# Products of constants in unused rows of a PSUM bank, at the end of positions in which TensorE has little to do

## The reference

```python
h = _L0_tok_ref(x, L0_tok_W)
h = h + _L0_attn_ref(_layernorm(h), ...)   # Toeplitz mixing along the sequence, by FFT
h = h + _L0_ffn_ref(_layernorm(h), ...)    # product keys -> k, v; then causal attention
h = h + _L1_attn_ref(_layernorm(h), ...)   # one head of full attention
h = h + _L1_ffn_ref(_layernorm(h), ...)    # 8 experts, top 2
```

```python
k = jnp.einsum('bnhk,bnhkd->bnhd', kv_scores, keys_table[ind])
v = jnp.einsum('bnhk,bnhkd->bnhd', kv_scores, values_table[ind])
sim = jnp.where(causal, jnp.einsum('bihd,bjhd->bhij', q, k), neg)
out = jnp.einsum('bhij,bjhd->bhid', softmax(sim), v)
```

## Time and profile before

| | |
|---|---|
| median of 3 runs | 3515.86 us (3515.56 to 3523.73) |
| profiled execution | span 4054.8 us; no other time of this execution is recorded, and nothing is recorded around the span |
| TensorE busy, products | 3145.7 us, 78% of the span, 9980 records |
| VectorE busy | 2896.5 us, 71% |
| ScalarE busy | 2063.6 us, 51% |
| GpSimd busy | 2009.3 us, 50% |
| granted clock of TensorE, mean | 0.865 |

### The profile page before, as it was taken

How to read it: one execution, slowest core, us unless ns; L and a number is a source line. 1 busy time by engine, 2 the same in 40 slices (tenths; PEclk the granted TensorE clock), 3 DMA queues, 4 the chain that set the end, 5 groups by cost and what they waited for, 6 DMA issues and landing times.

```text
span 4054.8 us, 40659 instructions
## 1 busy us (share of the span) xinstructions
PE 3145.7 (78%) x9980; PEld 1450.3 (36%) x9980; DVE 2896.5 (71%) x9977; ACT 2063.6 (51%) x4521; POOL 2009.3 (50%) x2084
## 2 busy tenths in 40 slices
PE   4895165687878787988887777889786778787898
PEld 2452022243434242433343333334343333333434
DVE  5435877778787777787788787877878787864423
ACT  3112145555555555555557565556585646555422
POOL 3000166666666665555555565565555565655200
PEclk9997577897989897988989888989888989888887
DMA  0121012121212121212121211111111212111000
GB/s 13 40 70 29 28 45 65 42 63 43 63 43 64 42 62 40 62 41 59 38 57 44 56 51 52 49 53 50 50 49 46 58 47 56 46 55 41 21 3 3
DMA packets 87160, 186.50 MB, mean 46 GB/s; under 512 B 40231, under 2 KB 42188, under 8 KB 86926
## 3 DMA queue, kind: packets, MB, share of 16 engines
q0 software_dynamic: 66560, 135.40, 12.7%
q1 hardware_dynamic: 20366, 48.53, 3.8%
HBM read 182.74 MB, written 1.05 MB: 45 GB/s over the span
## 4 chain that ended last, share of the span: by engine, by line
DVE 38%; PE 25%; issue 10%; another core or an unknown queue 9%; ACT 7%; DVEq 0%; ACTq 0%
DVE mx_W L1455 8%; PE mx_acc L1098 6%; PE mx_O L1110 5%; DVE mx_KVs L1623 4%; PE mx_area L1144 3%; ACT mx_GT L1360 3%; DVE mx_mx_part L1643 2%; PE mx_D L1088 2%; ACT mx_W L1292 2%; DVE mx_hot L1589 1%; DVE mx_mx L1643 1%; DVE mx_hot L1588 1%; DVE mx_S L1473 1%; DVE mx_row L1591 1%
## 5 line engine op out<-in xcount | busy, mean ns | idle before, releaser
L1070 POOL DMA_INDIRECT mx_G<-in_kv_table,mx_slot_i x2048 | 1977.6, 966 | 1781.5 <-DVE mx_W L1455 646.6
L1098 PE MATMUL mx_acc<-mx_W,mx_table 128*128 128x512 f32 x2048 | 1198.4, 669 | 0.4 <-ACT mx_kvT L1299 0.4
L1455 DVE SCALAR_TENSOR_TENSOR mx_W<-mx_D,mx_W 128x512 f32<-128x512 f32 x1024 | 704.2, 688 | 482.2 <-remote 221.3
L1292 ACT ACTIVATE mx_W<-mx_D 128x512 f32<-128x512 f32 x1024 | 607.0, 593 | 528.9 <-PE mx_D L1088 251.2
L1360 ACT ACTIVATE mx_GT<-mx_G,mx_slot_w 128x128 f32<-128x128 f32 x2048 | 758.5, 494 | 17.7 <-DVE mx_KVs L1623 13.4
L1088 PE MATMUL mx_D<-mx_U,mx_pick_b 96*128 96x512 bf16 x1024 | 437.7, 427 | 163.1 <-DVE mx_W L1455 127.3
L1098 PEld LDWEIGHTS mx_acc<-mx_W,mx_table 128*128 128x128 f32 x2048 | 443.0, 218 | 197.9 <-issue 119.5
L1316 ACT ACTIVATE mx_PT<-mx_area 128x512 f32<-128x512 f32 x480 | 247.5, 516 | 456.0 <-PE mx_area L1148 120.8
L1110 PE MATMUL mx_O<-mx_PT,mx_KVs 128*65 128x512 f32 (+3 forms) x768 | 333.7, 518 | 106.8 <-ACT mx_OT L1308 72.5
L1124 PE MATMUL mx_area<-mx_KTa,mx_QTa 64*128 64x512 f32 (+3 forms) x384 | 207.4, 625 | 229.0 <-DVE mx_mx_part L1643 138.2
L1623 DVE TENSOR_REDUCE mx_KVs<-mx_GT 128x128 f32<-128x2048 f32 x128 | 291.8, 2280 | 7.3 <-ACT mx_GT L1360 6.6
(11 more groups left out here) (350 smaller groups left out, 4604.3 us busy)
## 6 DMA issues: line engine op xcount, KB each, us to landing
mx_table<-in_kv_dense SPq DMA_DIRECT2D x64, 512.0 KB
mx_G<-in_kv_table,mx_slot_i POOLq DMA_INDIRECT x2048
cv_table<-in_c_idft SPq DMA_DIRECT2D x12, 512.0 KB, 3.2
cv_table<-in_c_dft SPq DMA_DIRECT2D x6, 512.0 KB, 3.3
cv_table<-in_c_idft SPq DMA_DIRECT2D x4, 256.0 KB, 3.2
out_h<-mx_xc SPq DMA_DIRECT2D x4, 256.0 KB
mx_G<-in_c_pick SPq DMA_DIRECT2D x1, 528.0 KB
st_h<-in_tok_W,em_ids POOLq DMA_INDIRECT x32
```

Source lines behind the costliest of these rows:

```text
L1070: pool.indirect_dma_start(G[g % RING][:, r, :], None, a["kv_table"], bass.IndirectOffsetOnAxis(slot_i[n % 2][:, k, r:r + 1], 0))\
L1098: pe.matmul(acc[:, :], table[:, tile, :], W[c % TILE_RING][:, :], start=(tile == 0), stop=(tile == TILES - 1)).then_inc(applied, 1)
L1292: act.activation(W[c % TILE_RING][:, :], D_ps[c % 3][:, :], ACT.Exp).then_inc(p_done, 1)
L1455: dve.scalar_tensor_tensor(W[c % TILE_RING][:, :], D_ps[c % 3][:, :], 0.0, W[c % TILE_RING][:, :], ALU.is_ge, ALU.mult).then_inc(w_done, 1)
```

## The change

A function `streamed(cnt, q)` adds up, from the timetable alone, how many columns TensorE streams in position `q` (a bfloat16 product of 512 columns counts 512, a float32 one 4 x 512). At the end of each position of slots 1 to 16, the new `spare_rows` then issues as many products of constants as bring that number near `STEADY` = 4800: `(4800 - streamed) // 512` of them, between none and four. Each has a constant of 96 rows by 32 columns as weights, streams 512 columns of another constant in bfloat16, and writes rows 96 to 127 of the bank `O_ps`, whose rows 0 to 64 hold the attention outputs. Nothing reads what they write. They wait for no semaphore and signal none.

```diff
+STEADY = 4800
...
+def streamed(cnt, q):
+    c = q - SLOT
+    total = 0
+    if 0 <= c + 3 < PAIRS * SLOT:
+        total += HALF * (2 if corner_of(tile_of(c + 3)[2])[3] else 1)
+    if 0 <= c < PAIRS * SLOT:
+        total += 4 * HALF
+    for use in area_uses(q - 2):
+        if use in cnt.weigh:
+            total += 4 * (HALF - piece(use)[2])
+    for use in area_uses(q)[:1]:
+        kind, _, _, r = use
+        if kind == "S":
+            total += 4 * ((r + 1) * P if r < 4 else HALF if r % 2 == 0 else ((r - 4) // 2 + 1) * P)
+        elif kind == "ST":
+            total += 4 * (HALF - piece(use)[2])
+        else:
+            total += 4 * HALF
+    key = cnt.x_at.get(divmod(q, SLOT))
+    if key is not None:
+        total += {"U": 8 * P, "post": 4 * P, "KK": 4 * P, "l1x": 4 * P, "l2x": 4 * P, "l2r": 4 * NB * E,
+                  "Y": 16 * (D + 1), "l1y": 16 * (D + 1)}.get(key[0], 4 * HALF)
+    return total
...
+            def spare_rows(count):
+                flat = pick_b[:, :, :].rearrange("p a c -> p (a c)")
+                for _ in range(count):
+                    pe.matmul(O_ps[96:P, :], pick_b[:, 0, 0:32], flat[:, 0:HALF], start=True, stop=True,
+                              skip_group_check=True)
...
                 if 0 <= c < PAIRS * SLOT and late:
                     apply_dense(c)
+                if 0 <= c < PAIRS * SLOT:
+                    spare_rows(max(0, STEADY - streamed(cnt, q)) // HALF)
```

## The result

| | before | changed |
|---|---|---|
| median of 4 runs | 3516.99 us | 3561.48 us |
| profiled execution, span | 3519.1 us (run `d1_before`, see below) | 3557.1 us |
| ratio of the times | | 1.0125, 95% interval 1.0112 to 1.0137 |
| TensorE busy | 2966.9 us, 84% | 3147.4 us, 88% |
| VectorE busy | 2888.9 us, 82% | 2891.6 us, 81% |

The change is 44.5 us slower. The prediction was 3500 us, 0.45% faster; the measured time is 1.5 us outside its range for 8 in 10 (3445 to 3560).

The account below looks back on a forecast made before the run. VectorE held 38% of the chain, TensorE 25%, with 847 us at half clock as target. Gain 40 less cost 27 gave -13 us, about -11 to -12 scaled, plus 4 us from earlier slot starts: 3500 us (8 in 10: 3445 to 3560).

Parts of the forecast that it names:

- Together 27 us: Cost of spare products on TensorE's chain: seven slots at 3.1 us make 22, the other eight at 0.6 make 5.
- I take off a fifth: 40 us: Gain from fuller clock in slots 2 to 16: 49 us, less a fifth because the clock falls behind pauses.
- -13: Net change in us on the profiled execution: 40 of clock gain against 27 of cost.
- scaled by 3515.86 / 4054.8 = 0.87: Whole kernel: the sum on the 4054.8 us profiled execution, times 0.87 for timed runs, about -11 to -12 us.
- so a further one costs (1.25 - 0.38) / 4 = 0.218 us at full clock: TensorE's time per spare product, from existing 512-column products of constants; 1067 of them make 232 us.
- The weight load of 98 ns is hidden in this pace, and the new one has 32 columns, not 128: Spare products on TensorE: weight loading adds nothing; by the skill's rule exposed cost would rise some 12 us.
- 11 x 0.218 x 0.16 = 0.4 us: Cost per slot in third quarters: 11 products, with TensorE on the chain for 16%.
- 32 x 0.218 x 0.034 = 0.2 us a slot: Cost in second quarters: about 32 products, TensorE on the chain for 3%, VectorE setting the pace.
- The first quarters' term: First quarters of slots 2 to 6, 10 and 14: 34 products, TensorE 34% of chain, 2.5 us a slot.
- Rival D: Slower: products expose TensorE's catching up in first quarters of slots 2 to 6, 10, 14; 3546 us (3527 to 3575), chance 0.28.
- Rival C: Nothing: clock ignores 32-column products, or is near full in timed runs and products sit in waits; 3510 to 3526 us, chance 0.12.
- Rival B: Large gain: ScalarE and VectorE follow TensorE's half-clock lateness, products fall into waits; 3455 us (3430 to 3475), chance 0.15.

Follow-up runs that it names:

- d1_before: The kernel before, repeated without edit for its profile on a chip without pauses: 3520.9 us, mean clock 0.913.

## Why the prediction was wrong

**The step that failed: the balance of "Together 27 us" of cost and "I take off a fifth: 40 us" of gain.** The cost took TensorE's share of the chain as the share of the products that is exposed. Without pauses, by the table above, 142 of some 297 us fell into waits and some 155 did not, 24 of them in slot 1, 49 in the first quarters, 47 in the second and 35 in the third. The gain was larger than forecast too, some 107 us, but smaller than this cost: +48 in place of -13. In the chain itself the spare products stand with 142 us where the prediction had 27. The direction of the clock was right: 32 columns of weights do hold it, as expected from the earlier trace rows (slot 1 from 0.80 to 0.95). But it gives back most where TensorE had waits to fill, and there it is not the engine that is waited for.

**The base: the sum "is made against the 4054.8 us of the profiled execution and then scaled by 3515.86 / 4054.8 = 0.87".** That most of the difference is pauses, and that the timed runs lack them, was right, but to scale a sum by 0.87 supposes that what stays keeps its proportions. It does not. Without the pauses the time at half clock is 382 us and not 847, and TensorE holds 38% of the chain and not 25%. This is not what turned the sign: on chips with the pauses, the kind that the rows come from, the forecast was -13 us, and the change measured +31, its first quarters alone +30 and +23 where the prediction has 17.5 us of cost and 7 x 26 x 0.34 / 2 = 31 of gain.

**The price: "so a further one costs (1.25 - 0.38) / 4 = 0.218 us at full clock" and "The weight load of 98 ns is hidden in this pace, and the new one has 32 columns, not 128".** The pace, 0.216 us, was right. What the row with five idle products couldn't show was the switch: those have 128 columns, as their neighbours have. 0.19 us a group, 67 us in 352 groups, is a term that was missing, 29% on top of the 232 us. It was part of the loss only where TensorE had no wait to fill, and what it cost the kernel by itself was not measured without pauses. The prediction set the Trainium skill (TensorE: Matmul & The Clock Gate, Part 3) aside because one row had the load hidden. Its rule, no overlap unless the row group differs, is not what the runs show either: with 96 or 128 columns nothing is exposed, with 32 and 64 it is when the neighbours are wider, and a product with 32 columns behind another one, in the same rows, starts 0.216 us after it.

**The exposure: third quarters "11 x 0.218 x 0.16 = 0.4 us", second quarters "32 x 0.218 x 0.034 = 0.2 us a slot".** In proportion these terms were mis-sized most: 6 us for all third quarters, which grew by 19 to 27 us, 1.3 to 1.8 a slot, since TensorE holds half of their chain, mostly at full clock; the earlier trace rows had 16%, with 30% in pauses. The second quarters, 3 us, grew by 2 to 9, and 41 us of spare products stand in their chain. The first quarters' term, 7 x 2.5 = 17.5 us, looks like the 16.4 that they grew by, but that is chance: the 17.5 are before the clock's gain and the 16.4 are after it, and 54 us of spare products stand in their chain. That slot 1 neither costs nor gains was right.

**Rival D** had the sign, the place of a part of it and nearly the size (3546, range to 3575), but by luck in part: its mechanism, that the light positions after the heavy quarter are where TensorE catches up, fits the chips with pauses (+30 and +23 us for the first quarters alone), while without pauses the products of positions 8 to 12 by themselves cost 4 us and the third quarters, which it left out, hold as much of the loss as the first or more. **Rival C** failed on its first ground, since the clock follows; its second, that without pauses the clock is nearer to full, was true (0.913). **Rival B** is out.

What stays open: a run of the third quarters alone and one of full-width products without pauses, why the third quarters cost nothing on chips with pauses, why 1067 short products cost as much as full ones where 352 cost a quarter, and what makes the pauses. No version that was run beats the kernel before; the nearest, the third quarters alone and slot 1 alone, both on chips with pauses, are within its noise and gain nothing.

## What to carry to other kernels

A clock that is not full is worth its price only where the engine at half clock is also the one that the others wait for; read the chain at the clock's low places first, and expect such filler products to cost their full time wherever that engine runs back to back, even in a position that looks light on paper. An engine's share of the chain is not the share of added work that is exposed: work added to an engine's program puts it on the chain. Here, filler with weights of 32 or 64 columns among wider ones cost some 0.1 us at either end of each group. And look whether the profile's span agrees with the timed runs: if it is 15% off, its shares describe another kind of execution, and here one factor did not mend them.

## What was not expected of the hardware

- At full clock a product with 32 or 64 columns of weights starts 520 ns after the second record of a float32 product with 128 columns, where one with 65, 96 or 128 columns starts after 428; and the next product with 128 columns starts 311 to 312 ns after a narrow one of 512 columns, where it would after 215. The two gaps are 92 and 97 ns. Products with 32 columns follow each other at 216 ns. The rows of the weights do the same: before the change (`d1_before`) the score blocks of L1124, with 64 rows and 128 columns, start 520 ns after a tile's product at the earliest, and what follows them 521 to 523, all 93 times at full clock, while 65 rows have 428. So a gap was there at either side of these score blocks before:

```profile
1240.79 0.59 PE L1124 MATMUL mx_area<-mx_KTb,mx_QTb 64*128 64x512 f32 x1
1241.31 0.39 PE L1088 MATMUL mx_D<-mx_U,mx_pick_b 96*128 96x512 bf16 x1
```

- Narrow products count for the clock: with 32 of 128 columns slot 1 went from 0.80 to 0.95.
- The same program takes 3517 us on some chips and 4050 on others. In the chains of the latter there are 86 to 112 pauses of over 1.5 us in each profile, with means of 3.6 to 4.2 us, in which the packets of the gathers went on, at 23 to 24 per us against 16 on average. The earlier trace rows is not typical: in the first profile all four engines were idle at the end of only 51 of its 100 pauses, for 1.6 us on average, and in the others one engine or more still worked. In 57 of the 100 it was ScalarE that had been idle longest. What ends these waits is not in the profile.
